# Half the columns for the second warm-up tiles, tokens turned by the centring matrix, and a shorter variance in a one-core metaformer block

## The reference

```python
x = x + conv_attention(ln_c(x))          # ln_c: over the 64 channels of each pixel, eps 1e-6
t = tokens(x)                            # one token of 64 values per pixel
t = t + mixture(ln_t(t))                 # 8 experts, 64 -> 256 -> 64, exact GELU, weights of the top two
x = images(t)
```

## Time and profile before

| | us |
|---|---|
| median of 3 runs | 123.01 |
| the three runs | 121.89, 123.01, 123.14 |
| profiled execution, its own time | 122.06 |
| its span | 120.3 |
| TensorE busy in the span | 115.6 (96%) |

### The profile page before, as it was taken

The page is one execution under the profiler, slowest core; times in us unless marked ns, Lnnn a source line. Parts: engine busy times, 40 slices in busy tenths (PEclk is TensorE's granted clock), DMA queues, the critical chain, the costliest instruction groups (busy, mean ns, idle before and its releaser), DMA issues.

```text
span 120.3 us, 3332 instructions
## 1 busy us (share of the span) xinstructions
PE 115.6 (96%) x1282; PEld 85.7 (71%) x1282; DVE 78.6 (65%) x267; ACT 70.0 (58%) x134; POOL 33.4 (28%) x51
## 2 busy tenths in 40 slices
PE   6999999999999889999999999999999999999990
PEld 5489956777888688969766876766766667666660
DVE  0489595843869989988990089977319064096972
ACT  4338799030696164578891994691963919739200
POOL 6637999991000003033340040000000000000370
PEclk9999999999999999999999999999999999999999
DMA  3679500000000000000000059911089780001001
GB/s 100 180 182 224 159 8 0 5 5 5 0 0 5 0 3 0 0 5 0 0 3 0 11 173 246 237 46 44 11 242 230 212 220 16 0 0 54 0 0 46
DMA packets 5460, 8.05 MB, mean 67 GB/s; under 512 B 1412, under 2 KB 3908, under 8 KB 5444
## 3 DMA queue, kind: packets, MB, share of 16 engines
q1 hardware_dynamic: 5344, 7.80, 25.3%
q10 hardware_dynamic: 100, 0.03, 0.2%
HBM read 7.24 MB, written 0.59 MB: 65 GB/s over the span
## 4 chain that ended last, share of the span: by engine, by line
PE 83%; DVE 9%; ACT 2%; issue 2%; POOL 1%; POOLq 1%; DVEq 0%
PE PS L996 36%; PE PS L1293 18%; PE PS L1112 13%; PE PS L1071 2%; DVE HEADWISE L898 2%; PE PS L1178 2%; PE PS L1081 2%; PE PS L1008 2%; PE PS L1217 1%; PE PS L1094 1%; PE PS L1203 1%; POOL XP L449 1%; PE PS L1024 1%; DVE XB L717 1%; PE PS L1248 1%
## 5 line engine op out<-in xcount | busy, mean ns | idle before, releaser
L573 ACT ACTIVATE MS<-PS,B 128x512 f32<-128x512 f32 x48 | 29.1, 690 | 7.2 <-PE PS L996 7.0
L996 PE MATMUL PS<-XS,W1H 128*128 128x512 f32 x64 | 26.6, 415 | 0.0
L996 PE MATMUL PS<-XS,W1L 128*128 128x512 f32 x64 | 25.3, 395 | 0.0
L1293 PE MATMUL PS<-MS,W 128*64 128x256 f32 x192 | 22.3, 383 | 0.0
L874 DVE SCALAR_TENSOR_TENSOR WY<-PS,B,HEADWISE 128x256 f32<-128x256 f32 x24 | 10.5, 480 | 14.8 <-PE PS L1293 14.4
L1293 PEld LDWEIGHTS PS<-MS,W 128*64 128x64 f32 x192 | 13.2, 137 | 8.5 <-ACT MS L573 1.5
L996 PEld LDWEIGHTS PS<-XS,W1H 128*128 128x128 f32 x64 | 12.0, 188 | 4.9 <-ACT MS L573 1.0
L1112 PE MATMUL PS<-HEADWISE,BANDS 32*32 32x448 f32 (+2 forms) x480 | 15.3, 564 | 0.0
L449 POOL TENSOR_TENSOR XP<-XP,WY 128x256 f32<-128x256 f32 x4 | 3.2, 808 | 41.1 <-DVE WY L924 40.8
L1112 PEld LDWEIGHTS PS<-HEADWISE,BANDS 32*32 32x32 f32 x480 | 10.3, 103 | 4.5 <-issue 1.5
L996 PEld LDWEIGHTS PS<-XS,W1L 128*128 128x128 f32 x64 | 12.1, 188 | 1.8
(11 more groups left out here) (135 smaller groups left out, 182.5 us busy)
## 6 DMA issues: line engine op xcount, KB each, us to landing
HEADWISE<-spread_dram SPq DMA_DIRECT2D x14, 256.0 KB, 5.0
W<-in_w_dram SPq DMA_DIRECT2D x3, 512.0 KB, 7.9
X<-in_x_dram SPq DMA_DIRECT2D x2, 256.0 KB, 3.2
HEADWISE<-spread_dram SPq DMA_DIRECT2D x4, 128.0 KB, 3.1
out_dram<-XP SPq DMA_DIRECT2D x4, 128.0 KB, 2.4
W<-spread_dram SPq DMA_DIRECT2D x2, 256.0 KB, 6.0
VEC<-in_vectors_dram SPq DMA_DIRECT2D x1, 132.0 KB
WQ<-in_w_qkv_dram SPq DMA_DIRECT2D x2, 48.0 KB, 3.0
```

The lines of the kernel that those rows point to most:

```text
L573: act.activation(hidden(n), PS[:, h_bank(n), :], ACT.Gelu, bias=B1[:, k:k + 1]).then_inc(gelu_done, 1)
L996: return pe.matmul(PS[0:parts, bank, cols[0]:cols[1]], lhsT, rhs, start=start, stop=stop)
L1293: i = pe.matmul(PS[C * b:C * b + C, bank, at:end], W2[:, KC * e + k, :], hidden(KC * (E * s + e) + k)[:, N * b:N * b + N], start=begins an ...
```

## The change

Three things. The second of the two batches of warm-up tiles streams 256 columns and not 512. The tokens are turned by a normal product with CEN as the moving operand in place of a transpose with the identity, so that what DVE reads is already centred; TensorE waits for CEN (`centre_made`) ahead of the tokens and for the identity (`ident_made`) behind them. As the mean of 64 centred values is zero, the means of their even and odd halves are opposite, and the variance is formed without the difference of the two: two steps that depend on each other and one that stands beside the first, where there were four instructions in three steps.

```diff
             dve.wait_ge(stats_done, 2)
-            dve.tensor_tensor(VAR1[:, 0, :], STATS[:, :, 1], STATS[:, :, 4], ALU.subtract)
-            link(dve.tensor_tensor(VAR1[:, 1, :], STATS[:, :, 2], STATS[:, :, 5], ALU.add))
-            link(dve.scalar_tensor_tensor(out=VAR1[:, 2, :], in0=VAR1[:, 0, :], scalar=0.25, in1=VAR1[:, 0, :],
-                                          op0=ALU.mult, op1=ALU.mult))
+            dve.tensor_tensor(VAR1[:, 1, :], STATS[:, :, 2], STATS[:, :, 5], ALU.add)
+            link(dve.tensor_tensor(VAR1[:, 2, :], STATS[:, :, 1], STATS[:, :, 1], ALU.mult))
             dve.scalar_tensor_tensor(out=VAR1[:, 3, :], in0=VAR1[:, 1, :], scalar=1.0 / C, in1=VAR1[:, 2, :],
                                      op0=ALU.mult, op1=ALU.add).then_inc(var_ready, 1)
...
-            def warm_up_tiles(height, columns):
+            def warm_up_tiles(height, width):
                 for row in range(128 // height):
+                    columns = width // (row + 1)
                     for col in range(4):
...
-                    i = pe.transpose(PS[:, STATS_BANKS[j // 2], 128 * (j % 2):128 * (j % 2) + 128],
-                                     pixel(j, slice(0, 128)), IDT[:, :])
+                    i = mm(STATS_BANKS[j // 2], (128 * (j % 2), 128 * (j % 2) + 128), pixel(j, slice(0, 128)), CEN[:, :], True, True)
...
             def centre_weights():
-                pe.wait_ge(centre_made, 1)
+                pe.wait_ge(ident_made, 1)
...
-            pe.wait_ge(ident_made, 1)
+            pe.wait_ge(centre_made, 1)
             turn_tokens(0)
```

## The result

The changed kernel takes 124.33 us in the median of 6 runs (123.31 to 124.58), the kernel before 122.64 (121.87 to 123.14, 6 runs): a ratio of 1.0144, 95% interval 1.0104 to 1.0185. Slower, by 1.7 us. The profiled execution took 123.87 us.

What follows compares the result with a forecast made beforehand. TensorE's serial path to the convolution bounds the kernel; tokens by matmul, less the tiles' gain, cost 0.71 us and the variance gains nothing. Adding 0.7 to the median 123.01 gives 123.7 us, 8-in-10 range 122.3 to 124.8.

Steps and rivals of the forecast that it cites:

- What bounds the kernel: TensorE's unbroken chain from the tokens to the convolution sets the time; whatever reaches the convolution late arrives late at the end.
- Warm-up tiles: TensorE ahead of the tokens: halving the second batch lets tokens start at 4.19 and not 4.51, gaining 0.32 of 0.43 us.
- Tokens by matmul: Eight one-pass transposes become eight two-pass products; the product with WQ starts at 6.65, not 5.94: loss 0.71 us, tiles' gain included.
- signs of being right: Product with WQ at 6.65, copy of RS ending at 8.2, R1 about 9.5, scaling from 10.3, convolution from about 16.0.
- Statistics and variance: DVE and ACT before the scaling: variance 0.1 us sooner, but root waits behind RS's copy; R1 stays at 9.5, gain nothing.
- After it nothing is late that could take the shift up: After the scaling nothing absorbs the delay; the 0.7 us shift goes through to the end.
- the line of 1%: Slower by 1.23 us, over 124.24: chance 0.12 from (b) and 0.13 from the forecast's upper end.
- (a): TensorE's clock rises sooner, as full passes replace transposes: 122.8 us, 0.2% under the median; chance 0.17.
- (b): TensorE's clock rises later after the halved batch, costing 0.48 us per us of delay, up to 125.4 us; chance 0.15.
- (c): Loss on TensorE is hidden and R1 decides the scaling: 122.7 us; chance 0.08 together with (d).
- (d): A product by CEN costs one pass, leaving only the tiles' -0.3 us: 122.7 us; chance 0.08 together with (c).

Runs made afterwards that it cites:

- second measurement: The changed kernel itself, measured again in a later session against the kernel before: 123.62 us (10 runs), ratio 1.0092 (1.0061 to 1.0123).

## Why the prediction was right, and where not

The range of 122.3 to 124.8 held the 124.33, and the main mechanism, extra passes on a serial path, was the forecast one. The number owes something to luck. The forecast was 0.7 us on top of 123.01, the median of three runs; over six runs it is 122.64. From there the same sum gives 123.3, and the measured shift of 1.7 us (1.1 in the second measurement) is well over 0.7. A base that was 0.37 us too high covered a part of two terms that were missing. By its steps:

*What bounds the kernel* was right: the path along TensorE is so rigid that from the product with WQ to the convolution lie 9.32 us before (5.94 to 15.26) and 9.31 after (7.45 to 16.76).

*Warm-up tiles* is the step that failed. "The first batch starts at 2.62 and the second at 3.48, so 512 columns take 0.86 us" took passes for batches. The gain of 0.32 us was 0.02. The rows before could not tell the two readings apart: both groups of eight records have the same form, and can be the two rows of the loop or the first and second passes of all eight tiles. The second reading should have been a rival.

*Tokens by matmul* was right in kind and in count, two passes for one. Its size was 0.71 us with the gain in it, hence 1.03 without. The traces give 8 x 0.11 = 0.88 at the full clock and 0.1 more for each further pass at the low one: 1.50 between the two profiled executions, seven of whose passes are the clock's draw, 0.68 between the profile of before and the changed kernel's second, in which the rise came sooner. That second profile comes close to all the signs of being right (the product with WQ at 6.63 for 6.65, R1 at 9.40 for 9.5, scaling at 10.32 for 10.3, convolution at 15.94 for 16.0), by two errors that cancel: the tokens start 0.30 us later than forecast, and only about two passes are low where the forecast had some five. Filler of the same number of passes cost 0.63%, 0.8 us. (In the forecast's list of starts the pass at 5.03, with a rise at 5.1, would take 0.14 us and not 0.18; nothing hangs on it.)

*Statistics and variance*: the root behind the copy of RS, R1 ahead of the products, and the step's gain of nothing were all as forecast. R1 itself was not at 9.5 but at 10.21 in the first profile, as `rs()` came 1.5 us later with the late rise and not 0.7; TensorE was later by as much, so nothing came of it. What I had no term for is the step's loss: with one instruction less on DVE it idles 0.35 us more, a hundred microseconds later. "After it nothing is late that could take the shift up" was right, but something was added.

The sum: 0.9 to 1.0 us of passes and 0.35 of DVE's wait are 1.2 to 1.3 us, 1.0 to 1.1%, where the two measurements gave 1.44% and 0.92%; up to half a microsecond of the first is left over. The forecast was 0.7 us, 0.6%: two missing terms of a third of a microsecond each, the tiles' gain that wasn't there and DVE's wait. They took the first measurement over the line of 1% to which I gave 0.25, and the second near it.

*Rivals.* (a) didn't come: the time rose, and the moment of the rise is spread in both families. With products by CEN and at least one full batch it came between about 4.9 and 6.6 us; with transposes at 5.1 in the profile of before, about 6.6 in the one with the tiles alone, and before the tokens, which start at 4.33, in the one with the short variance. Of (b) the change itself shows nothing (full and halved tiles are alike); it may hold where both batches are halved. (c) and (d) are out by R1's 0.9 us of lead and by the sixteen passes.

What stays open: why the changed kernel was 1.44% slower in one session and 0.92% in the other (the intervals overlap), whether both batches halved delay the clock, by their columns or by the gap behind them, and whether DVE's longer idle time is the fetch of its code.

## What to carry to other kernels

Where a serial engine's program is the critical path, filler on it isn't slack: anything added ahead shifts all behind, and when the waits change, the filler has to be counted anew. Before halving one of several array tiles, look whether they run one after the other or side by side; only the longest sets the end. And a saved instruction off the path is worth nothing by itself, and can cost, as the 0.35 us here, at a place far behind it: compare the idle times of an engine far from the edit as well. Last, add a forecast shift to a base of more than three runs when the runs spread by more than the shift.

## What the runs showed of the hardware

TensorE's rise from 1.2 to 2.4 GHz comes at another moment in each execution of the same program: of the 18 passes up to WQ about ten were low in one and two in another, and that made 0.8 us of the time. The Trainium skill, "TensorE: Matmul & The Clock Gate" (Part 1), says the same, that the transition moves from run to run; a profile's first microseconds are thus one draw, and the granted clock of the window view, 1.00 from the start, doesn't show it.

DVE's idle time at one place depends on how many instructions its program has: 1.07 us with 267 and 1.42 with 266, in all fourteen traces. The Trainium skill, "Runtime: NRT & Kernel Launch" (Terms, the row on IRAM), says that an engine's instruction memory is refilled in blocks; the two packets of 0.01 MB beside the wait fit that. No run here shows that the wait is such a refill.
